# Attention scores and row maxima in 64-row array tiles, issued in pairs, with other products in bursts at a step's end

## The reference, cut to what matters

```python
# first attention: 16 heads of width 16, causal
scores = jnp.einsum('bhqd,bhkd->bhqk', q, k) / sqrt(d_k) + mask
attn = jax.nn.softmax(scores, axis=-1)
out = jnp.einsum('bhqk,bhkd->bhqd', attn, v)
# second attention: 32 heads of width 8
att = jnp.einsum('bqhd,bkhd->bhqk', q, k) / np.float32(np.sqrt(hd))
p = jax.nn.softmax(att, axis=-1)
o = jnp.einsum('bhqk,bkhd->bqhd', p, v).reshape(B, S, D) @ wo + x
```

## Time and profile before

| | |
|---|---|
| three runs, median (lowest, highest) | 1882.75 us (1882.68, 1887.67) |
| the profiled execution, its own time | 1884.22 us |
| its span from first to last instruction | 1882.5 us |
| PE busy, share of the span | 1641.7 us, 87% |
| DVE, ACT, POOL busy | 1178.9, 1026.1, 450.0 us |
| mean granted PE clock | 0.949 of full speed |
| loop body, start of its first scores product to that of the next | 218.5 us in the third of six |

### The profile page before, as it was taken

How to read it: one execution, slowest core, us unless ns; L and a number is a source line. 1 busy time by engine, 2 the same in 40 slices (tenths; PEclk the granted TensorE clock), 3 DMA queues, 4 the chain that set the end, 5 groups by cost and what they waited for, 6 DMA issues and landing times.

```text
span 1882.5 us, 32284 instructions
## 1 busy us (share of the span) xinstructions
PE 1641.7 (87%) x8677; PEld 649.4 (34%) x8721; DVE 1178.9 (63%) x3093; ACT 1026.1 (55%) x1967; POOL 450.0 (24%) x797
## 2 busy tenths in 40 slices
PE   4477699998999989999899989999899998889878
PEld 2123222344323533335223443235333352214315
DVE  3556298654895558864786548955587648775430
ACT  0044436664576545765566646765557645666561
POOL 0133323123132222231232221321222313210100
PEclk8688979999999989999899999999899999999998
DMA  6650333423233332332333232333333223221301
GB/s 172 165 147 13 108 84 108 113 77 98 74 117 108 91 92 83 95 98 71 92 115 106 77 119 53 117 111 88 92 99 88 88 71 88 63 57 48 102 2 56
DMA packets 126614, 171.54 MB, mean 91 GB/s; under 512 B 17048, under 2 KB 102872, under 8 KB 122848
## 3 DMA queue, kind: packets, MB, share of 16 engines
q1 hardware_dynamic: 126432, 169.33, 31.1%
HBM read 110.67 MB, written 56.66 MB: 89 GB/s over the span
## 4 chain that ended last, share of the span: by engine, by line
PE 63%; DVE 15%; issue 9%; ACT 6%; DMA 4%; SPq 1%; POOL 1%; DVEq 1%; ACTq 0%; POOLq 0%
PE bank_out L1071 13%; PE bank_max L1033 11%; PE bank_scores L1055 10%; DVE neg_max L1264 7%; PE bank_side L1001 7%; PE bank_side L1161 6%; PE bank_side L1014 4%; PE bank_misc L1145 3%; PE bank_side L1145 3%; ACT probs L863 3%; DMA q_stack<-max_parts 2%; PE bank_misc L1080 2%; PE bank_side L1126 2%; PE bank_misc L1116 1%; DVE normed L1224 1%
## 5 line engine op out<-in xcount | busy, mean ns | idle before, releaser
L863 ACT ACTIVATE probs<-bank_scores 128x512 f32<-128x512 f32 (+3 forms) x1536 | 793.3, 543 | 632.0 <-PE bank_scores L1055 617.9
L1264 DVE TENSOR_REDUCE neg_max<-bank_max 128x1 f32<-128x512 f32 x1024 | 667.2, 681 | 299.0 <-PE bank_max L1033 297.5
L1033 PE MATMUL bank_max<-k_stack,q_stack 64*128 64x512 bf16 (+4 forms) x1505 | 520.0, 376 | 89.5 <-issue 31.2
L1055 PE MATMUL bank_scores<-q_stack,k_stack 64*128 64x512 bf16 (+4 forms) x1523 | 528.0, 371 | 61.6 <-ACT probs L863 39.8
L1071 PE MATMUL bank_out<-probs,v_tile 128*9 128x512 f32 (+4 forms) x3072 | 371.4, 557 | 2.7 <-issue 1.5
L1261 DVE CUSTOM_DVE_ANT_0 bank_max<-bank_max,causal 128x384 f32<-128x384 f32 (+3 forms) x512 | 246.5, 506 | 167.4 <-PE bank_max L1033 147.4
L1033 PEld LDWEIGHTS bank_max<-k_stack,q_stack 64*128 64x128 bf16 (+1 forms) x1536 | 134.9, 96 | 577.7 <-issue 405.5
L1055 PEld LDWEIGHTS bank_scores<-q_stack,k_stack 64*128 64x128 bf16 (+1 forms) x1536 | 135.4, 95 | 273.8 <-ACT probs L863 142.8
L774 POOL TENSOR_SCALAR_AFFINE_SELECT probs<-probs 128x512 f32<-128x512 f32 x128 | 81.0, 634 | 371.9 <-ACT probs L863 371.9
L756 POOL CAST max_parts<-max_row 16x128 bf16<-16x128 f32 x96 | 26.8, 279 | 577.3 <-DVE max_row L1275 577.0
L1161 PE MATMUL bank_side<-w_out,hidden_T 128*128 128x256 f32 x512 | 133.8, 388 | 13.6 <-ACT hidden_T L899 10.7
(11 more groups left out here) (113 smaller groups left out, 1333.0 us busy)
## 6 DMA issues: line engine op xcount, KB each, us to landing
q_stack<-q_parts SPq DMA_DIRECT2D x16, 1024.0 KB, 6.2
q_stack<-q_parts SPq DMA_DIRECT2D x64, 256.0 KB, 4.1
w_in<-in_L_ffn_w_dram SPq DMA_DIRECT2D x16, 1024.0 KB, 6.0
w_out<-in_L_ffn_w_dram SPq DMA_DIRECT2D x16, 1024.0 KB, 8.5
q_parts<-partsq SPq DMA_DIRECT2D x32, 384.0 KB, 2.6
k_parts<-partsk SPq DMA_DIRECT2D x32, 384.0 KB, 2.6
k_stack<-k_parts SPq DMA_DIRECT2D x32, 384.0 KB, 8.8
k_stack<-k_parts SPq DMA_DIRECT2D x64, 192.0 KB, 4.4
```

The costliest lines, as they stand in the source:

```text
L863: nc.scalar.activation(probs[s % 2][:, k, q0:S], region[bank][:, q0:S], ACT.Exp, scale=float(WIDTH[a]) ** -0.5).then_inc(drained[bank], 1)
L1033: pe.matmul(region[bank][:, 0:keys], q_stack[buf][rows, at, qt * P:(qt + 1) * P], k_stack[buf][rows, at, 0:keys], start=True, stop=True).t ...
L1055: pe.matmul(region[bank][:, q0:S], k_stack[buf][rows, at, kt * P:(kt + 1) * P], q_stack[buf][rows, at, q0:S], start=True, stop=True).then_ ...
L1264: v.tensor_reduce(dst, region[bank], AX_X, ALU.max).then_inc(drained[bank], 1)
```

## The change

Both layers now use two tiles of 64 rows. A sixteen-wide head is computed in two passes of 64 rows (`PASSES = (2, 1)`) that accumulate in the same bank. `maxima` and `scores` on PE do nothing at an even slot beyond waiting for the bank, and at the odd slot issue both heads of the pair, one in each tile (`head_at` pairs heads 0 and 2, then 1 and 3). A step becomes two halves: maxima pair, scores pair, then whatever is placed there. The values product of an eight-wide step stands in the first half of the next step, that of a sixteen-wide step in the second half (`VALUES_SLOT = (3, 1)`). Side items are issued whole (`place_together`) at the end of a step, behind the second pair. The stack loads become four DMAs of queries and four of keys for a=0, in place of one and two.

```diff
-TILES = (1, 2)
-TILE_ROWS = (128, 64)
+TILES = 2
+TILE_ROWS = 64
+PASSES = (2, 1)
...
-VALUES_SLOT = 3
-ROWS_AFTER = 2
-ROWS_SLOT = 1
-NORMALISE_SLOT = 2
+VALUES_SLOT = (3, 1)
+ROWS_AFTER = 1
+NORMALISE_AFTER = 2
+LAST_SLOT = 3
...
+def head_at(k):
+
+    return k // 2 + k % 2 * (GROUP // 2)
...
+        for half in (range(2), range(2, SLOTS)):
+            for k in half:
+                if p < len(lead) and k not in early:
+                    out.append(("maxima", *lead[p], k))
+                early.discard(k)
+            for k in half:
+                if p < len(main):
+                    out.append(("scores", *main[p], k))
+            ready = [item for k in half for item in waiting.pop((p, k), [])]
+            out += sorted(ready, key=lambda item: item[0] != "values")
...
+def place_together(plan, ats, items):
+
+    for at, item in zip(ats, items, strict=True):
+        plan.setdefault(at, []).extend(in_pieces(*item))
...
+        items += [("values_early",), ("maxima_early", 0), ("maxima_early", 1)]
         for n in range(2, 4):
-            plan[start + 3] += [*in_pieces("expert_in", off, j, n), ("gelu", off, j, n)]
+            items += [*in_pieces("expert_in", off, j, n), ("gelu", off, j, n)]
+        items += [("maxima_early", 2), ("maxima_early", 3)]
...
+        out = in_pieces("expert_out", off, j)
+        for step, few in enumerate((out[:3], out[3:6], out[6:])):
+            plan.setdefault(start + (step + 1) * SLOTS, []).extend(few)
...
-    place_pieces(beside, (40, 44, 48, 52), qk_items(0, 2))
+    place_together(beside, (47, 51, 55, 59), qk_items(0, 2))
...
-        stack_dmas = [1 + 2, 1 + 2, 2 + 2, 2 + 2, 2 + 2, 2 + 2]
+        stack_dmas = [4 + 4, 4 + 4, 2 + 2, 2 + 2, 2 + 2, 2 + 2]
...
                 start_fill(f[0], turn)
-                first, at = tile_of(a, k) * TILE_ROWS[a], column_of(a, g, k)
-                rows = slice(first, first + TILE_ROWS[a])
-                pe.matmul(region[bank][:, q0:S], k_stack[buf][rows, at, kt * P:(kt + 1) * P], q_stack[buf][rows, at, q0:S],
-                          start=True, stop=True).then_inc(filled[bank], 1)
                 scores_fill[s % 2] = f[0]
+                if k % 2 == 0:
+                    pair_bank["scores"] = bank
+                    return
+                for i in range(PASSES[a]):
+                    for kk, to in ((k - 1, pair_bank["scores"]), (k, bank)):
+                        rows, at = tile_rows(kk), column_of(a, g, i, kk)
+                        last = i == PASSES[a] - 1
+                        ins = pe.matmul(region[to][:, q0:S], k_stack[buf][rows, at, kt * P:(kt + 1) * P],
+                                        q_stack[buf][rows, at, q0:S], start=(i == 0), stop=last)
+                        if last:
+                            ins.then_inc(filled[to], 1)
```

More of the change, by code:

```diff
@@ L78, in attention @@
 def attention(main, lead, beside, handed=(), hand_on=None):
-    out, waiting = [], {at: [item] for at, item in handed}
+    out, waiting = [], {}
+    for at, item in handed:
+        waiting.setdefault(at, []).append(item)
     count = max(len(main), len(lead))
@@ L86, in attention @@
     for p in range(count):
-        for k in range(SLOTS):
-            if p < len(lead) and k not in early:
-                out.append(("maxima", *lead[p], k))
-            early.discard(k)
-            if p < len(main):
-                off, a, s = main[p]
-                out.append(("scores", off, a, s, k))
-            out += waiting.pop((p, k), [])
-            for item in beside.pop(p * SLOTS + k, []):
-                if item[0] == "maxima_early":
-                    if p + 1 < len(lead):
-                        early.add(item[1])
-                        out.append(("maxima", *lead[p + 1], item[1]))
-                elif item[0] == "values_early":
-                    early.add("values")
-                    out.append(("values", *main[p]))
-                else:
-                    out.append(item)
+        for half in (range(2), range(2, SLOTS)):
[8 more added lines that the diff above has]
+            out += sorted(ready, key=lambda item: item[0] != "values")
+            for k in half:
+                for item in beside.pop(p * SLOTS + k, []):
+                    if item[0] == "maxima_early":
+                        if p + 1 < len(lead):
+                            early.add(item[1])
+                            out.append(("maxima", *lead[p + 1], item[1]))
+                    elif item[0] == "values_early":
+                        early.add("values")
+                        out.append(("values", *main[p]))
+                    else:
+                        out.append(item)
         if p < len(main) and "values" in early:
@@ L694, in _ @@
             for n in range(3):
-                for t in range(TILES[1]):
-                    rows = slice((t + 1) * TILE_ROWS[1] - P // SLICES, (t + 1) * TILE_ROWS[1])
+                for t in range(TILES):
+                    rows = slice((t + 1) * TILE_ROWS - P // SLICES, (t + 1) * TILE_ROWS)
                     sp.dma_start(k_stack[n][rows, :, :], ones.unsqueeze(1).broadcast_to([P // SLICES, UNIT_HEADS, S]))\
@@ L1029, in maxima @@
                 start_fill(f[0], turn)
-                kk = turned(k)
-                first, at = tile_of(a, kk) * TILE_ROWS[a], column_of(a, g, kk)
-                rows = slice(first, first + TILE_ROWS[a])
-                pe.matmul(region[bank][:, 0:keys], q_stack[buf][rows, at, qt * P:(qt + 1) * P],
-                          k_stack[buf][rows, at, 0:keys], start=True, stop=True).then_inc(filled[bank], 1)
-                maxima_fill[g] = f[0]
+                maxima_fill[g] = f[0]
+                if k % 2 == 0:
+                    pair_bank["max"] = bank
+                    return
+                for i in range(PASSES[a]):
+                    for kk, to in ((k - 1, pair_bank["max"]), (k, bank)):
+                        rows, at = tile_rows(kk), column_of(a, g, i, kk)
+                        last = i == PASSES[a] - 1
+                        ins = pe.matmul(region[to][:, 0:keys], q_stack[buf][rows, at, qt * P:(qt + 1) * P],
+                                        k_stack[buf][rows, at, 0:keys], start=(i == 0), stop=last)
+                        if last:
+                            ins.then_inc(filled[to], 1)
             def max_rows(b, turn, f, a, g):
```

118 lines of the change are left out of this document (56 added, 62 removed).

## The result

| | before | after |
|---|---|---|
| median of the runs, us | 1882.72 | 1940.57 (1923.38 to 1945.28, four runs) |
| ratio | 1 | 1.0284, 95% interval 1.0218 to 1.0351 |
| the profiled execution, us | 1884.2 | 1937.8 |
| its span, us | 1882.5 | 1936.1 |
| PE busy, us | 1641.7 | 1530.3 |

A forecast was written before the change was run, and what follows sets the result against it. PE's stream bounds steps with large side items; bare steps wait for ACT's exponentials. 1884.2 - 15.6 (six turns) + 4 (ahead of the loop) - 10.2 (behind) = 1862 us, range 1812 to 1897.

The forecast's parts named there:

- Removed from PE's stream: Whole kernel: PE's stream shrinks by 17.2 us a turn and 8 behind the loop, grows by 3 ahead of it.
- The round: Each half step of a bare a=1 step: product, gaps and two exponentials take 1.6 us, so 3.2 a step.
- The 32 a=1 steps: Eight-wide steps of a loop turn: 125.6 us in place of 131.8, so -6.2 a turn.
- layer norm pieces: I take 2: In a turn's a=1 steps: layer norm pieces between reductions cost nothing to 5 us; 2 was taken.
- The 16 a=0 steps: Sixteen-wide steps of a loop turn: 90.3 us in place of 86.7, so +3.6 a turn.
- The expert's end: `expert_out` waits behind a scores pair held by ACT's table load: two first halves 2.6 for 0.87, 3.5 us a turn.
- Ahead of the loop: The 19 a=0 steps before the loop: four widths sum to 11.9 for 10.7; +4 us, bounds 0 and +8.
- Behind the loop: Steps after the loop: first window -7.4, ten expert steps 62.7 for 66.0, bare ones +1.5; in all -10.2 us.
- DVE starves behind every burst, slower: Rival: other bursts and layer norm steps also cost late maxima pairs of 0.3 to 0.6; 1898 to 1934 us, chance 0.20.
- Weight loads: Rival: two passes double the loads of a=0 and lengthen passes; +55 us, 1917, chance 0.05.
- Clock: Rival: more short waits lower the granted clock, under 0.95 in the loop; 1882 us, no difference, chance 0.06.
- heads running one after the other: Rival: two heads of one product do not run together, 0.22 twice every half step; far over 1900 us, chance 0.02.

The follow-up runs named there:

- e10: The changed kernel with the edits of e1, e4, e8 and e6 together: 1815.37 us, 0.9643 of the kernel before.
- e5: The kernel before, with all pieces of each large side item issued together in one slot: 1903.10 us, 1.0098.
- e12: e5 with DVE's reductions put ahead of the subtraction behind a projection burst: 1900.47 us, 1.0108.
- e2: The changed kernel with only the scores products issued singly, maxima still in pairs: 1916.55 us, 1.0192.
- e4: The changed kernel with DVE's subtraction of a `qk` item moved behind the next two reductions: 1920.05 us, 1.0217.
- e1: The changed kernel with every maxima and scores product issued as soon as its own bank is free: 1889.82 us, 1.0049.
- e8: The changed kernel with the first two pieces of `expert_out` moved ahead of the scores pair that waits for the table: 1904.71 us, 1.0118.
- e9: The changed kernel with the edits of e1, e4 and e8 together, two passes and bursts kept: 1844.82 us, 0.9802.
- e3: The changed kernel with only the maxima products issued singly, scores still in pairs: 1930.39 us, 1.0260.
- e11: e10 with the two `ffn_sum` items of a step moved half a step earlier into the empty first half: 1809.67 us, 0.9611.
- e6: The changed kernel with sixteen-wide heads back in the full array in one pass, stack loads as before: 1920.59 us, 1.0204.
- e7: The changed kernel with the edits of e6 and e1 together: 1866.54 us, 0.9922.

## Why the prediction was wrong

The forecast sum was -15.6 (loop), +4 (ahead), -10.2 (behind). The profiled executions have +37.2, +22.1 and -5.7, together the 53.6 between them. The mechanisms were named, most of them with a size that was too small. Some 6 us of the loop's miss are a matter of the base: the third turn of the kernel before, 218.5, stood for all six, whose mean is 217.5.

- **Removed from PE's stream.** True as a count: 108 were forecast, and PE is busy 111 us less. As a time it was worth something only where PE was the bound. e10, with 81 us less busy PE than before, is 67 us faster. So the saving is real and comes out once the added waits are gone. Which part of the new order carries e10's gain no run isolates. The bursts by themselves lose (e5, e12); a candidate is that two maxima products, and then two scores products, now stand side by side.
- **The round.** The bare step was forecast at 3.2 and took 3.28 in the loop, 3.34 behind it. The round is 1.64 for 1.6: the release takes 0.16 for a pair where I carried over the 0.05 of a single product, while ACT starts 0.40 after the product's start where I had 0.46. e2 has the step back at 3.00. The Trainium skill, TensorEngine Tiling (Array Packing), section PSUM Bottleneck, says that emptying PSUM can become the limit once tiling has sped up TensorE. The trace agrees that the banks are the limit, but not through the rate at which they are emptied (ACT has 0.55 idle in each round): both banks are filled together and freed together.
- **The 32 a=1 steps: -6.2, measured -1.2 a turn.** This is the first step of the sum that failed, 30 us over six turns. Plain burst steps came as forecast, 4.11 for 4.05. Steps 13 to 15, each behind a `qk` burst, were 4.63, 4.92 and 4.53 for 4.6, and with e4 they are 4.28, 4.50 and 4.28, so DVE's order is a cause. What failed is "layer norm pieces: I take 2", and that nothing stood there for steps with `normalise` on PE and for the turn's start. By medians, step 6 took 6.02 for 4.7, step 16 took 4.36 for 3.2, and steps 1, 2, 10, 17, 24 and 32 each took 0.4 to 1.0 more than before. In step 16 PE stands 1.43 for a maxima pair. With the edits of e1, e4 and e8, the part is at 126.4 in e9 and 126.0 in e10. That is near the forecast's 125.6, but for a kernel whose products are issued singly, so it doesn't bear the forecast out.
- **The 16 a=0 steps: +3.6, measured +7.4 a turn.** The window was to be near 90 and is 93.0 on the mean. Steps 33 to 38 came nearly as forecast (24.5 for 23.7). The expert's end is the second step that failed. PE's wait there was 2.13 where I had some 2.4, so that size was right, and from it I had 3.5 a turn; steps 40 and 44 lost 2.9 and 2.35, and e8 gives back 5.1 in the a=0 part. What the sum lacked is what comes behind the wait: a stretch at the lower clock in which the twelve following products run at 0.38 each. Where the clock stayed up, the two steps took 5.63 to 5.85, and the forecast's terms give 2.6 + 3.2 = 5.8; the eight of twelve where it fell took 1.2 to 1.7 more. Step 39 lacked a term as well, 12.1 for 1.2 + 9.9 = 11.1.
- **Ahead of the loop: +4, measured +22.1.** The third, and the largest against its size; even the upper bound of 8 was far under. I had bounded only the 19 plain a=0 steps, which cost 5.6. The start, which I hadn't counted, cost 6.1: it is at 99.7, and at 92.3 in e3 with single maxima. The time up to the very first maxima product differs by some 4 us between traces of the same work (74.5 in e10, 79.0 in e11). From that product to the first step it is steady: 15.4 us before, 23.8 in all four kernels with pairs of maxima and two passes, 17.3 with single maxima and two passes (e1, e3, e9), 19.6 in e6, 15.4 in e7 and e10. So the pairs cost 6.5 there and two passes 1.9. The 32 steps cost 16.0, of which two passes with their stack loads and the pairs are 10.8 (e7 has 165.2); the rest isn't told apart.
- **Behind the loop: -10.2, measured -5.7.** The first window came at 125.4 for 120.7, the 14 bare steps at +3.5 for +1.5. Of the 5.7, 4.9 were gained behind the start of the very last step, for which the forecast had no term, so it is luck: the clock was at its upper level there, and in the trace of the kernel before it wasn't. These are the windows, before and then after:

```profile
1826.50:1882.50 56.00, 43.07 (x172) 29.45 (x168) 3.31 (x6) 11.94 (x24) 2.52 (x2) 0.87 0.14 47
```

```profile
1885.00:1936.10 51.10, 37.26 (x168) 27.09 (x168) 3.32 (x6) 11.95 (x24) 2.53 (x2) 1.00 0.16 52
```

It goes with the clock and not with this change: the same stretch takes 51.1 in e10 and 56.0 in e11, at 1.00 and 0.88. To the last step's start the change was worth only 0.8 behind the loop.

Of the rivals, **"DVE starves behind every burst, slower"** came true in kind: the time lies past its 1934, and waits for DVE's reductions are the largest that grew. But its mechanism explains a part only: all pair waits together are 51 us (e1), with ACT's share larger than DVE's (24 against 10 taken alone, the 10 not clear of noise), and the expert's end and the two passes are causes of their own. **Weight loads** fell: the loads of a pair start together, and a load is still 94 to 95 ns. The groups on the page after:

```profile
L1052 PEld LDWEIGHTS bank_max<-k_stack,q_stack 64*128 64x128 bf16 x2048 | 82.6, 94 | 639.5 <-DVE neg_max L1291 273.9
L1081 PEld LDWEIGHTS bank_scores<-q_stack,k_stack 64*128 64x128 bf16 x2048 | 105.3, 95 | 244.8 <-ACT probs L877 151.6
```

They are busy 188 us for 4096 loads, less than the 387 that loads one behind another would take. **Clock** was put at 0.06 as a cause by itself. The loop's clock is 0.965, over the 0.95 that was to decide, so by that sign it isn't the cause. But that sign was too coarse: before, it was 0.979, and by the two means (over all six turns) PE spent 94 us at its lower level in place of 55. The eight falls at experts' ends cost 13 of the loop's 37.2 us; what the other added time at the lower level cost isn't shown. In e10, with the waits mended, it is 52 us again. So the clock is a part of the cause, as what the waits bring with them. The chances had a slip of their own: the 0.02 for heads running one after the other, far over 1900, was added on the side of faster, which so stood at 0.63 in place of 0.61. One reason lies behind many of the misses: a pair's wait was costed where it shows in a bare step, and left out in steps where another engine's item comes late.

## What to carry to other kernels

Joining two products that need two separate buffers turns two short waits into one wait for the later buffer: write them next to each other in the order, so that they share the array when both are free, but let each wait for its own bank. When work is grouped, list for each engine what now stands in front of the instruction that frees a buffer: here a subtraction in front of reductions, and a pair in front of a product whose input was ready. Costs ahead of a loop, where other work doesn't hide them, need a term of their own.

## What the runs showed of the hardware

**A wait can be paid again in the clock, but isn't every time.** At 895.02 PE went idle for 2.13 us; it then ran at its lower level (1.2 GHz; 0.77 over the stretch of 7.4 us). In the fourth turn it went idle for the same 2.13 and stayed at its upper level (2.4 GHz; 1.00). In the kernel before, the waits at this place were 0.89 and 0.39 and the clock stayed at 1.00:

```profile
854.20:858.50 4.30, 3.02 (x15) 1.73 (x13) 0.00 (x0) 3.04 (x7) 0.00 (x0) 1.00 0.56 182
```

In e8 the waits were 0.35 and 0.57, and the clock stayed at 1.00 behind all twelve. Behind waits of 2.13 and 2.34 it fell 8 times of 12 in the kernel after and 4 of 12 in e4; behind 1.87 and 2.09 in e1, 3 of 12. What decides between two waits of the same length isn't shown, and no kernel here waits between 0.89 and 1.87 at this place. It also spreads the times of one kernel: the four runs of the kernel after, from 1923 to 1945 us, have mean clocks of 0.952, 0.944, 0.943 and 0.939 in that order.

**A DVE operation on 128x4 elements took 0.92 us.** Step 16 in the kernel after, timeline of DVE, PE and POOL:

```profile
792.40 0.92 DVE L1222 TENSOR_TENSOR root<-root 128x4 f32<-128x4 f32 x1
793.24 1.27 DVE L1291 TENSOR_REDUCE neg_max<-bank_max 128x1 f32<-128x512 f32 x2
794.44 0.14 DVE L1224 SCALAR_TENSOR_TENSOR rstd<-root,rstd 128x4 f32<-128x4 f32 x1
```

```profile
793.98 0.39 PE L1052 MATMUL bank_max<-k_stack,q_stack 64*128 64x512 bf16 x2 [1.43 <-DVE neg_max L1291]
```

```profile
792.15 1.15 POOL L754 TENSOR_TENSOR partsk<-rest,partsk 128x512 bf16<-128x512 f32 x1
```

The first one ends at 793.32, as POOL's operation does at 793.30. The one at 787.87 above ended at 788.79, and POOL's there at 788.78. Beside an idle POOL both forms, L1222 and L1224, take 0.14 to 0.16. The Trainium skill, SBUF — State Buffer, section SBUF: two separate sides, says that a DVE operation with two inputs in SBUF and a GpSimd operation that reads it exclude each other for the whole instruction. The ends of these two pairs agree with it. It was there before the change too: of the 216 operations on 128x4 at the three lines L1220, L1222 and L1224, 37 took over 0.3 us, and 12 of the same 216 before; a POOL operation ended with each of them. But a maxima pair that waits behind such an operation makes PE stand 1.43 us, and the forecast had no term for it. No run took it away by itself.

**The table load needs nothing more than its 1.28 us.** GELU ends at 895.25, the load runs from 895.26 to 896.54, and the exponential starts at 896.56.
